# A selective-scan kernel: a new order for the preparation of the next chunks on TensorE and ScalarE

## The reference

```python
xs, z  = split(x @ in_w.T)                      # 256 -> 2 x 512
xc     = silu(cb + causal_conv4(xs, cw))
dt, B, C = split(xc @ xp_w.T)                   # 16 + 16 + 16
delta  = softplus(dt @ dt_w.T + dt_b)
h_t    = h_{t-1} * exp(delta_t * A) + delta_t * xc_t * B_t      # 512 x 16 states
y_t    = sum over states of h_t * C_t, plus xc_t * D_skip
x      = layer_norm((y * silu(z)) @ out_w.T + x)
```

## The kernel before, in words

| work | PE at slot | ACT at slot |
|---|---|---|
| convolution of block 3 of chunk g+1, `convolve` (L508) | 0 | 1 (`copy_conv`, then `tanh_xc`, `silu_z`) |
| `project_x` (L515), `project_dt` (L524) for g+1 | 2; 3, 4 | 3; 4, 5 (then `sigmoids`, `polynomial`) |
| `project_out` (L534, L536) of chunk g-1, bank 0 and bank 1 | 5, 6 | 6, 7 (`copy_out`, L737) |
| z of g+1, `project_in(.., 1)` (L498) | 8, 9 | 9, 10 (`copy_z`, L732) |
| x of g+2 transposed, `transpose_x` (L488) | 10 | 11 (`copy_xT`, L649) |
| xs of g+2, `project_in(.., 0)` (L498) | 11, 12 | 12, 13 (`copy_xs`, L666) |
| convolution of blocks 0 to 2 of g+2 (L508) | 13, 14, 15 | 14, 15 and 0 |

## Time and profile before

### The profile page before, as it was taken

How to read it: one execution, slowest core, us unless ns; L and a number is a source line. 1 busy time by engine, 2 the same in 40 slices (tenths; PEclk the granted TensorE clock), 3 DMA queues, 4 the chain that set the end, 5 groups by cost and what they waited for, 6 DMA issues and landing times. The chain is left out here.

```text
span 8296.2 us, 75437 instructions
## 1 busy us (share of the span) xinstructions
PE 6530.6 (79%) x21028; PEld 2528.0 (30%) x21028; DVE 7849.2 (95%) x7411; ACT 5545.2 (67%) x9589; POOL 6983.9 (84%) x3444
## 2 busy tenths in 40 slices
PE   5777777787778777787777877887777877775888
PEld 2222222232223222222222322232222322222555
DVE  8999999999999999999999999999999999996776
ACT  5676776777766776667766777667766777663444
POOL 3898889988898888988899888988889888985555
PEclk8989899989989899898999889898999888987999
DMA  6454454444554454554545445454555445451110
GB/s 181 116 118 109 104 127 115 117 115 113 127 118 110 100 121 115 120 122 108 126 115 117 105 109 126 116 125 103 121 119 119 109 104 122 115 118 52 39 38 30
DMA packets 566028, 909.25 MB, mean 110 GB/s; under 512 B 58368, under 2 KB 200192, under 8 KB 564352
## 3 DMA queue, kind: packets, MB, share of 16 engines
q1 hardware_dynamic: 565632, 904.73, 45.7%
HBM read 715.55 MB, written 188.94 MB: 109 GB/s over the span
## 5 line engine op out<-in xcount | busy, mean ns | idle before, releaser
L905 POOL TENSOR_TENSOR hc<-h,crep 128x1024 f32<-128x1024 f32 x2048 | 4782.2, 2360 | 714.3 <-PE acc L474 633.4
L1033 DVE TENSOR_TENSOR_SCAN h<-dA,carry,bu 128x512 f32<-128x512 f32 x3072 | 3755.0, 1264 | 0.4 <-ACT carry L638 0.4
L1018 DVE TENSOR_TENSOR bu<-durep,B_all 128x1024 f32<-128x1024 f32 x2048 | 2480.8, 1211 | 188.2 <-PE B_all L456 168.2
L629 ACT ACTIVATE dA<-drep,cur 128x512 f32<-128x512 f32 x4096 | 2618.7, 711 | 0.6 <-DMA drep<-delta_dram 0.3
L456 PE MATMUL B_all<-dtc,spread_b 128*128 128x512 f32 x2048 | 1308.0, 724 | 1460.8 <-DVE bu L1018 1458.5
L638 ACT COPY carry<-h 128x4 f32<-128x4 f32 x1023 | 199.4, 195 | 1713.0 <-DVE h L1033 1711.6
L474 PE MATMUL acc<-hc,gather 128*32 128x512 f32 x8192 | 1284.9, 703 | 5.5 <-POOL hc L905 5.5
L1033 DVE TENSOR_TENSOR_SCAN h<-dA,bu 128x512 f32<-128x512 f32 x1024 | 1192.4, 1203 | 6.9 <-ACT dA L629 6.8
L498 PE MATMUL work<-xT,inw 128*128 128x512 f32 x2048 | 1119.6, 697 | 93.1 <-ACT xT L649 82.7
L456 PEld LDWEIGHTS B_all<-dtc,spread_b 128*128 128x128 f32 x2048 | 360.0, 208 | 2144.9 <-DVE bu L1018 2057.0
L508 PE MATMUL work<-xs,taps 128*128 128x512 f32 x2048 | 950.3, 607 | 0.0
(11 more groups left out here) (179 smaller groups left out, 6807.8 us busy)
## 6 DMA issues: line engine op xcount, KB each, us to landing
drep<-delta_dram SPq DMA_DIRECT2D x1024, 256.0 KB, 6.4
durep<-du_dram SPq DMA_DIRECT2D x1024, 256.0 KB, 7.2
crep<-c_dram SPq DMA_DIRECT2D x1024, 64.0 KB, 6.7
delta_dram<-za SPq DMA_DIRECT2D x64, 1024.0 KB, 4.2
du_dram<-relu SPq DMA_DIRECT2D x64, 1024.0 KB, 5.3
x_res<-xbuf SPq DMA_DIRECT2D x64, 512.0 KB, 3.8
xbuf<-x_res SPq DMA_DIRECT2D x64, 512.0 KB, 5.4
xc<-xbuf SPq DMA_DIRECT2D x63, 512.0 KB, 4.3
```

What stands on the lines that cost most here:

```text
L629: act.activation(dA[:, 4 * (s % 2) + k, :], drep[q % 2][:, k, :], ACT.Exp, scale=cur[:, p_, 4 * s + k:4 * s + k + 1]).then_inc(da_ready, 1)
L905: pool.tensor_tensor(hc[:, pair, :], h[:, pair, :], crep[:, j:j + 1, :].to_broadcast([P, 2, T]), ALU.mult).then_inc(hc_ready, 1)
L1018: dve.tensor_tensor(bu[:, 2 * k:2 * k + 2, :], durep[q % 2][:, 2 * k:2 * k + 2, :], B_all[:].unsqueeze(1).to_broadcast([P, 2, T]), ALU.mul ...
L1033: dve.tensor_tensor_scan(h[:, r, :], dA[:, r, :], bu[:, k, :], start, ALU.mult, ALU.add).then_inc(scanned, 1)
```

## The change

z of chunk g+1 is projected at slots 7 and 8 and copied at 8 and 9. x of g+2 is transposed at 9 and copied at the head of ACT's slot 10, ahead of the exponentials. xs is projected at 10 and 11 and copied at 11 and 12. The four convolutions stand at 12 to 15, so none is left for slot 0 of the next turn; their copies stand at 13, 14, 15 and 0. `tanh_xc` and `silu_z` move on ACT from slot 1 to slot 0, and POOL's `silu_xc` from slot 2 to slot 1. The skip term no longer opens its quarter: the first sums write acc (start=True), and the skip term is added at the second, fourth, second and second state group of its quarter, on PE at slots 3, 9, 11 and 15. The load of x waits for state group 7 in place of 4, and the load of skip for three counts more. The fillings of the two banks are counted from a list that `place` builds.

```diff
+    SKIP_AT = (1, 3, 1, 1)
...
             def load_x(n):
                 c = ready(n % CH)
                 if n >= 2:
-                    sp.wait_ge(summed, 2 * (NG * (n - 2) + QS) + 1)
+                    sp.wait_ge(summed, 2 * (NG * (n - 2) + 2 * QS - 1) + 1)
...
-                    sp.wait_ge(summed, 2 * NG * n - 6)
+                    sp.wait_ge(summed, 2 * NG * n - 3)
...
-                if positive(DB * n + q):
-                    pe.wait_ge(acc_read, DB * n + q)
-                pe.matmul(acc[:], skip[:, q, :], xc[:, p_, q, :], start=True, stop=False, skip_group_check=True)
+                pe.matmul(acc[:], skip[:, q, :], xc[:, p_, q, :], start=False, stop=False, skip_group_check=True)
...
-                if s % QS == 0:
-                    skip_term(n, p_, s // QS)
+                q = s // QS
+                if s % QS == 0 and positive(DB * n + q):
+                    pe.wait_ge(acc_read, DB * n + q)
+                if s % QS == SKIP_AT[q]:
+                    skip_term(n, p_, q)
                 for k in range(4):
...
-                    ins = pe.matmul(acc[32 * k:32 * k + 32, :], gather[:], hc[:, 4 * (s % 2) + k, :], start=False,
+                    ins = pe.matmul(acc[32 * k:32 * k + 32, :], gather[:], hc[:, 4 * (s % 2) + k, :], start=s % QS == 0,
...
-                        if s == 0:
-                            convolve(nxt, 3)
...
-                        if s in (8, 9):
-                            project_in(nxt, 2 * (s - 8), 1)
-                            project_in(nxt, 2 * (s - 8) + 1, 1)
+                        if s in (7, 8):
+                            project_in(nxt, 2 * (s - 7), 1)
+                            project_in(nxt, 2 * (s - 7) + 1, 1)
                         if not (isinstance(g, int) and g == TOT - 2):
-                            if s == 10:
+                            if s == 9:
                                 transpose_x(g + 2)
-                            if s in (11, 12):
-                                project_in(g + 2, 2 * (s - 11), 0)
-                                project_in(g + 2, 2 * (s - 11) + 1, 0)
-                            if s in (13, 14, 15):
-                                convolve(g + 2, s - 13)
+                            if s in (10, 11):
+                                project_in(g + 2, 2 * (s - 10), 0)
+                                project_in(g + 2, 2 * (s - 10) + 1, 0)
+                            if s >= 12:
+                                convolve(g + 2, s - 12)
...
+                    if s == 10 and not is_last(g) and g < TOT - 2:
+                        copy_xT(g + 2)
                     exp(group(g, s + 1), here if s + 1 < NG else other)
```

More of the change, by code:

```diff
@@ L69, in mamba_layers @@
     C_DB, C_CB = 0, DB
+    SKIP_AT = (1, 3, 1, 1)
+    FILL_BANK = {"xp": 0, "dt0": 1, "dt1": 0, "dt2": 1, "dt3": 0, "out0": 0, "out1": 1, "tr0": 0, "tr1": 1}
+    FILL_BANK.update({f"{name}{e}": e % 2 for name in ("z", "xs", "c") for e in range(4)})
     xv = xbuf.rearrange("(c t p) d -> c p t d", t=NT, p=P)
@@ L190, in is_last @@
             return isinstance(g, int) and g == TOT - 1
[L192 to L212, removed]
-        def fill(b, n, name):
[L216 to L220, removed]
@@ L222, in mamba_layers, with place, place_head @@
-        LAST_OUT = (fill0(TOT, "out") + 1, fill1(TOT, "out") + 1)
+        fill_at, filled = {}, [0, 0]
+        def place(n, *names):
+            for name in names:
+                b = FILL_BANK[name]
+                fill_at[b, n, name] = filled[b]
+                filled[b] += 1
+        def place_head(n):
+            place(n, "tr0", "tr1", "xs0", "xs1", "xs2", "xs3", "c0", "c1", "c2", "c3")
+        place_head(0)
+        place(0, "xp", "dt0", "dt1", "dt2", "dt3", "z0", "z1", "z2", "z3")
@@ new lines, in mamba_layers @@
+        place_head(1)
+        for n in range(1, TOT + 1):
+            if n < TOT:
+                place(n, "xp", "dt0", "dt1", "dt2", "dt3")
+            if n >= 2:
+                place(n - 2, "out0", "out1")
+            if n < TOT:
+                place(n, "z0", "z1", "z2", "z3")
+            if n < TOT - 1:
+                place_head(n + 1)
+        place(TOT - 1, "out0", "out1")
+        def fill(b, n, name):
+            return fill_at[b, n, f"{name}{b}" if name in ("tr", "out") else name]
@@ L224, in out_fill @@
         def out_fill(b, m):
-            if isinstance(m, int) and m == TOT - 1:
-                return LAST_OUT[b]
-            return fill(b, m + 2, "out")
+            return fill(b, m, "out")
         def group(g, s):
@@ L571, in _ @@
             turn_piece(2)
-            for e in range(3):
+            for e in range(DB):
                 convolve(1, e)
@@ L818, in _ @@
             copy_piece(2)
-            for e in range(2):
+            for e in range(3):
                 copy_conv(1, 1, e)
@@ L833, in turn @@
                         if s == 0:
-                            copy_conv(n, other, 2)
+                            copy_conv(n, other, 3)
                             take_params(n, other)
-                        if s == 1:
-                            copy_conv(n, other, 3)
                             tanh_xc(n, other)
-                    if s == 1:
+                    if s == 0:
                         if is_last(g):
@@ L857, in turn @@
                     if not is_last(g):
-                        if s == 9 and is_first(g):
+                        if s == 8 and is_first(g):
                             act.wait_ge(weights_saved, 48)
-                        if s in (9, 10):
-                            copy_z(n, other, 2 * (s - 9))
-                            copy_z(n, other, 2 * (s - 9) + 1)
+                        if s in (8, 9):
+                            copy_z(n, other, 2 * (s - 8))
+                            copy_z(n, other, 2 * (s - 8) + 1)
                     if not is_first(g):
@@ L869, in turn @@
                         if not (isinstance(g, int) and g == TOT - 2):
[L870 to L875, removed]
+                            if s in (11, 12):
+                                copy_xs(g + 2, (ph + 2) % 4, 2 * (s - 11))
+                                copy_xs(g + 2, (ph + 2) % 4, 2 * (s - 11) + 1)
+                            if s == 12:
                                 keep_halo(g + 2)
                                 take_biases(g + 2, here)
-                            if s in (14, 15):
-                                copy_conv(g + 2, here, s - 14)
+                            if s >= 13:
+                                copy_conv(g + 2, here, s - 13)
                     if not is_first(g):
@@ L974, in turn @@
                     if not is_last(g):
-                        if s == 2:
+                        if s == 1:
                             silu_xc(g + 1, other)
```

## The result

The changed kernel takes 8350.19 us (median of 4 runs, 8348.4 to 8353.3) against 8296.22 for the kernel before in the same comparison: a ratio of 1.0065, 95% interval 1.0048 to 1.0083. The forecast was 8345, slower by 0.6%. The profiled execution has a span of 8348.7 us.

A forecast was written before the change was run, and what follows sets the result against it. DVE, busy 95% of the span, was taken as the bound, losing 168.2 us waiting for B_all. 8298.0 us + 24 (chunks) + 25 (layer changes) = 8347, median 8345 us, +0.6%; range 8205 to 8430.

The forecast's parts named there:

- What goes: Waits for B_all at slots 3, 9 and 12 (0.49, 0.25, 1.38 us) go; 0.3 us taken for slot 3.
- Slot 8: z's second projection waits for a bank copy_out frees; B_all queued behind it is late: new wait of 0.7 us.
- Slot 10: x is loaded later; transposes and the B_all behind them run at the low clock: wait 1.6 us, bounds 0 and 2.5.
- Slot 11: Sums and two xs projections, partly at the low clock, delay B_all: wait 0.3 us, bounds 0 and 1.7.
- Changes of layer: At three chunks in-projection weights land behind x, drep and durep, making xs and B_all late: 25 us in all.
- The sum of the waits and the half that comes through: Per chunk 2.9 us of waits against 2.1; half or less comes through: +0.4 us on 61 chunks, +24 us.
- Everything else is covered: First-turn conv3, earlier silu and tanh, the skip load and skip terms at turns 11 and 15 all fit in slack.
- Rival 1: Full clock holds, slots 3, 10 and 11 cost nothing, only slot 8's 0.7 us stays: 8198 us; chance 0.22.
- Rival 2: Evening-out is complete, a chunk stays at 116.05 us, only the layers cost: 8321 us; chance 0.18.
- rival 3: x lands 1 us later than taken, paid at slot 10 in each chunk: 8408 us; chance 0.11.
- rival 4: Low clock at slot 8 while z1 waits for its bank, 2.9 us more per chunk: 8524 us; chance 0.07.

The follow-up runs named there:

- z spread: x early, plus z's four blocks projected one at slot 7, two at 8, one at 9: 8259.49 us.
- PE kept busy: Changed kernel with four extra unused matmuls ahead of the transposes of x: 8296.03 us.
- x early: Changed kernel with quarter 1's skip term at its second state group and the load of x waiting for state group 5, not 7: 8259.84 us.
- skip alone: Kernel before with only the skip terms moved, each to its quarter's second state group, x load at group 5, skip load three counts later: 8295.37 us.
- the variance later: z spread with POOL's variance instructions behind its slot 11 product (first version, 8212.66 us) or at slots 12 to 15 (second, 8207.97 us).
- du cut: POOL's du product on 64 of 2048 columns: changed kernel 8276.33 us; kernel before 8258.42 us; skip alone 8237.67 us.
- slot 1 busy: skip alone with du cut, plus four unused matmuls on PE at slot 1: 8283.12 us.

## Why the prediction was right, and where it was not

The direction and the size came out, 8350 for 8345, and both of its parts did, though part of the size by luck: 58 ordinary chunks at 116.56 - 116.05 = +0.51 us are +30 us (forecast +0.4 on all 61, +24), and three layer changes are 373.3 - 3 x 116.05 = +25 (forecast 25). By its own steps:

- **What goes.** Slot 12's wait and slot 9's went, as said. At slot 3, 0.07 us is left (forecast 0.3). The skip term's leaving is not enough for that: with it alone slot 3 kept 0.74, for want of the earlier silu.
- **Slot 8.** 0.67 us (forecast 0.7), behind the bank that copy_out frees. z spread, which takes the bank away, took the wait away.
- **Slot 10.** x is issued 5.4 us into slot 9 (3828.69 less the slot's start, 3823.25; forecast 5.4) and lands 4.4 us later. The wait is 1.38 us (forecast 1.6), and "PE kept busy" shows that without the low clock nearly nothing of it is left. In the changed kernel the granted clock was at the level of 1.2 GHz after PE had stood still for 4.5 us; with matmuls there it stayed at that of 2.4 GHz. The Trainium skill has it ("TensorE: Matmul & The Clock Gate", section "Part 4: PE-mode transpose") that transposes do not bring the full clock. The rows agree that B_all behind them is slow after an idle stretch, and it was so in each of the 62 chunks, at 1.88 us in the mean. No run here shows that the transposes fail to count: with the clock up ahead of them it stayed up over their 1.09 us and the B_all behind, and an idle stretch of 4.40 us without a slow transpose (x early) ended in a slow B_all too.
- **Slot 11.** Nothing in the ordinary chunks (forecast 0.3); the 0.44 us of the table is the layers' wait.
- **Changes of layer.** 9.4, 9.7 and 7.7 us of waits at slot 11 in three chunks, each of which was to lose 8.3; together the three are 25 us longer. inw took 12.4 us from issue to landing (forecast 13).
- **The sum of the waits and the half that comes through** is the step that failed, in its mechanism. It counted B_all alone, 2.9 us for 2.1, and halved the difference by the earlier trace rows without knowing what does the halving. Measured, the B_all waits of the ordinary chunks fell, from 2.72 to 2.23 us. The new waits were 0.7 us too high in the forecast, and the old ones 0.6 too low: the sum set them against the 2.1 us of the one chunk that I read in time, though 168.2 / 62 = 2.7 stood in its first paragraph. What rose were waits that I had not priced: over the span durep by 58.6 - 18.6 = 40 us and dA by 13 us. B_all in the three chunks of the layers rose by 25 us, and elsewhere it fell by 28 (165.1 - 168.2 = -3 in all): -28 + 25 + 40 + 13 = 50 of the 52.5 us. That +0.4 us for an ordinary chunk came so near +0.51 is luck.

"Everything else is covered" was wrong for one path: product of du on POOL, store, load. Over chunks 2 to 62 the product ends, in us after the start of slot 13:

| | before | PE kept busy | after | x early | skip alone | z spread |
|---|---|---|---|---|---|---|
| end of the du product | 3.44 | 3.70 | 4.34 | 4.68 | 4.88 | 5.35 |
| wait for durep, slot 15 | 0.18 | 0.51 | 0.77 | 0.96 | 1.00 | 0.98 |
| all waits of slots 14 and 15 | 0.18 | 0.52 | 1.00 | 1.22 | 1.47 | 1.87 |

The wait for durep follows the end of the product until it is about 1 us; from there slot 14's waits for hc and dA take the rest. All of them together (last row) are the end of the product less 3.2 to 3.5 us, in each of the six kernels and in the first version of "the variance later" too (4.86 and 1.44), where durep alone is down to 0.32. The du cut shows the link by taking the wait away.

In the changed kernel the product is 0.9 us later. DVE is not earlier: it reaches slot 13 at 94.5 us of the chunk, as before (94.6), its new waits at slots 8 and 10 standing in for that of slot 12. It is POOL that is late, since PE's late sums hold it for 1.19 us in slot 10 and 0.31 in slot 11 (means over the chunks), where they held it for none. With PE kept busy, x as late but the clock high, the product ends 97.9 us into the chunk, as before (98.0), and in the changed kernel at 98.9. So this lateness too came with the low clock behind the late x.

Rival 1 (faster, full clock) failed at the point named, PE's idle time ahead of the transposes, but it was a near thing: the move of one skip term made 90 us of difference, and PE kept busy 54. Rival 2 (fully evened out) is excluded by the ordinary chunks: +30 us is beyond what a measurement takes for no change. x came when I said, against rival 3, and slot 8 kept the full clock, against rival 4.

**Open.** With du cut short, the chunk lengths in the order of the kernel before repeat, with period eight (112.8 to 116.6 us), and with period four with the skip terms (114.4, 114.3, 115.6 and 116.5 us), and in the latter slot 3 loses 1.88 us where it lost 0.74 with du in full. The run with slot 1 busy excludes the clock at slot 2. The traces say where the 1.1 us goes: POOL ends silu_xc 0.6 us later (21.8 us after the chunk's start, from 21.2), and project_x behind it takes 4.98 us in place of 4.31. Why POOL comes later there was not tried. Nor was any version with the store of du split in two, which might start durep's loads earlier.

## What to carry to other kernels

When a wait moves, read one row further than the engine that it names: list every product that crosses a chunk's boundary (here du: POOL, store, load, 15.6 us without POOL's part), with its slack, since a wait elsewhere in the chunk may be what covers it. A load whose go-ahead is a count of sums moves with every term that is put ahead of that count: the place of one skip term cost 90 us. Take the mean of a wait over all chunks, not one chunk, before it goes into a sum.

## What the runs showed of the hardware

- Work that nobody uses can pay on PE: four matmuls ahead of a late transpose made the kernel 54 us faster (8350.19 to 8296.03), because everything behind ran at 2.4 GHz (B_all 1.02 us) instead of 1.2 (1.91). At another place, ahead of an input that comes late, the same four cost 45 us (8237.67 to 8283.12), since PE only idled later, and the clock fell there, on a longer matmul group.
- A 1 MB load took 12.4 us from issue to landing with 2.5 MB issued just ahead of it on the same queue, and 4.9 us without them.
